# Attention block on one core: x kept in a ring of six buffers, gamma and beta rows broadcast by TensorE, the maxima pass one slot later over 65 rows, stacks without zero rows

## The reference

```python
def _sln(h, w, ln_g, ln_b, Wg, bg, Wb, bb):
    mu = jnp.mean(h, axis=-1, keepdims=True)
    var = jnp.mean((h - mu) ** 2, axis=-1, keepdims=True)
    ln = (h - mu) / jnp.sqrt(var + EPS) * ln_g + ln_b
    return (w @ Wg.T + bg)[:, None, :] * ln + (w @ Wb.T + bb)[:, None, :]
h = _sln(hidden, w, ...)                       # hidden: (16, 256, 256)
qkv = (h @ Wqkv.T + bqkv)                      # q, k, v: 16 heads x 16 features
energy = jnp.einsum('bhqd,bhkd->bhqk', q, k)
att = jax.nn.softmax(energy, axis=-1) / D ** 0.5
out = jnp.einsum('bhqk,bhkd->bhqd', att, v) ... @ Wp.T + bp
h1 = out + hidden
return _sln(h1, w, ...) + h1
```

## Time and profile before

| | |
|---|---|
| median of 3 runs | 408.3 us (407.98 to 411.03) |
| profiled execution | 412.25 us, its span 410.4 us |
| mean granted clock of TensorE | 0.967 |
| busy in the span | PE 88%, DVE 73%, ACT 57%, POOL 30% |
| DMA queue of SP | 53.11 MB, 78.7% of 16 engines |

### The profile page before, as it was taken

How to read it: one execution, slowest core, us unless ns; L and a number is a source line. 1 busy time by engine, 2 the same in 40 slices (tenths; PEclk the granted TensorE clock), 3 DMA queues, 4 the chain that set the end, 5 groups by cost and what they waited for, 6 DMA issues and landing times.

```text
span 410.4 us, 8984 instructions
## 1 busy us (share of the span) xinstructions
PE 359.5 (88%) x3208; PEld 300.6 (73%) x3209; DVE 298.1 (73%) x730; ACT 235.5 (57%) x437; POOL 121.6 (30%) x108
## 2 busy tenths in 40 slices
PE   3856579798989999998999899999899999988972
PEld 3636478687878788887878687878787888857652
DVE  7714738476878788786878787887787886977454
ACT  8320227466666767575657566665667575755750
POOL 5310403142415142332424242424142323030332
PEclk9986969899999999999999999999999999999996
DMA  6179895969598799969897969899979989590221
GB/s 206 37 96 127 116 106 103 162 100 161 115 174 114 157 158 128 186 108 181 119 192 109 180 112 180 126 175 121 174 123 124 168 108 181 101 184 10 81 78 51
DMA packets 50334, 53.68 MB, mean 131 GB/s; under 512 B 6610, under 2 KB 41825, under 8 KB 50290
## 3 DMA queue, kind: packets, MB, share of 16 engines
q1 hardware_dynamic: 50290, 53.11, 78.7%
HBM read 14.18 MB, written 4.23 MB: 45 GB/s over the span
## 4 chain that ended last, share of the span: by engine, by line
PE 49%; DMA 22%; SPq 18%; DVE 5%; issue 4%; ACT 1%; POOL 1%; POOLq 0%; DVEq 0%
DMA kst<-qk_l 19%; PE m L689 16%; SPq L288 15%; PE st L689 11%; PE sa L689 9%; PE pv L689 9%; DMA qst<-m_l 2%; SPq L291 2%; PE pv L784 2%; DVE mx L489 1%; DVE qst L640 1%; PE pv L837 1%; PE pv L798 1%; SPq L301 1%; DVE y L600 0%
## 5 line engine op out<-in xcount | busy, mean ns | idle before, releaser
L489 DVE TENSOR_REDUCE mx<-sa 128x2 f32<-128x512 f32 x256 | 174.3, 683 | 90.6 <-PE sa L689 86.3
L467 ACT ACTIVATE p<-st 128x512 f32<-128x512 f32 x256 | 150.5, 597 | 101.8 <-PE st L689 99.6
L689 PE MATMUL sa<-kst,qst 128*128 128x256 f32 x512 | 107.8, 294 | 31.9 <-DMA kst<-qk_l 31.1
L689 PE MATMUL st<-qst,kst 128*128 128x256 f32 x512 | 112.8, 303 | 1.4 <-ACT p L467 0.7
L689 PEld LDWEIGHTS sa<-kst,qst 128*128 128x128 f32 x512 | 80.5, 194 | 37.8 <-DMA kst<-qk_l 28.0
L689 PEld LDWEIGHTS st<-qst,kst 128*128 128x128 f32 x512 | 79.6, 193 | 23.2 <-ACT p L467 15.2
L689 PE MATMUL pv<-p,v_st 128*32 128x256 f32 x1024 | 68.5, 385 | 0.3 <-ACT p L467 0.3
L357 POOL TENSOR_TENSOR hT_l<-hT,hT_h 128x512 fp32r<-128x512 f32 x16 | 20.6, 1285 | 100.3 <-ACT hT_h L400 100.3
L371 POOL TENSOR_TENSOR rstd<-vare,minus_half 128x4 f32<-128x4 f32 (+1 forms) x21 | 18.8, 893 | 95.5 <-DVE vare L544 92.0
L376 POOL TENSOR_TENSOR h1b<-h,gb 128x512 f32<-128x512 f32 x16 | 20.6, 1285 | 87.2 <-DVE h L573 87.2
L689 PEld LDWEIGHTS pv<-p,v_st 128*32 128x32 f32 x1024 | 26.7, 109 | 20.2 <-ACT p L467 0.5
(11 more groups left out here) (95 smaller groups left out, 537.2 us busy)
## 6 DMA issues: line engine op xcount, KB each, us to landing
qst<-qk_h SPq DMA_DIRECT2D x64, 128.0 KB
qst<-qk_l SPq DMA_DIRECT2D x64, 128.0 KB
kst<-qk_h SPq DMA_DIRECT2D x64, 128.0 KB
kst<-qk_l SPq DMA_DIRECT2D x64, 128.0 KB
xa<-x_dram SPq DMA_DIRECT2D x16, 256.0 KB, 4.0
xd<-x_dram SPq DMA_DIRECT2D x16, 256.0 KB, 3.4
gb<-gb_rows SPq DMA_DIRECT2D x16, 256.0 KB, 3.7
out_dram<-y SPq DMA_DIRECT2D x16, 256.0 KB, 4.0
```

Of the source, the lines that this page charges most:

```text
L467: nc.scalar.activation(p32[:, h % PR, :], st_ps[h % 2][:], ACT.Exp).then_inc(exp_done, 1)
L489: dve.tensor_reduce(mx[:, par(a), h // HH, (h % HH) * TT:(h % HH + 1) * TT], sa_ps[h % 2][:].rearrange("p (t n) -> p t n", t=TT), AX.X, AL ...
L689: return nc.tensor.matmul(o, l, r, start=start, stop=stop)
```

## The change

- `xa` becomes a ring of six images (`NX = 6`, `xbuf(a)`). POOL adds the bias in it, DVE's L573 reads it, and the second load of x (`xd`) goes.
- The rows of gamma and beta stay on chip. They are split into a high and a low part in `gb_hl` (16 rows each). In slot 3 of a step (`S_GB`) PE multiplies them with `pick_b`, a 0/1 matrix that POOL makes for each image in its slot 2, into `pv_ps[0]`: the row, broadcast to 128 partitions. ACT copies it to `gb` in slot 4. POOL's `h1b` goes from slot 1 to slot 6, `xn` from slot 5 to 7. The DRAM round trip and the `gb` DMAs go.
- `LEAD` goes: slot h holds `scores_max(b+1, h)`.
- Row 64 of `qst` is zero for good and rows 65 and 66 hold the maxima. The maxima pass contracts over 65 rows, the scores pass over 67. So the clearing DMA goes (`NSTK = 8`), as do the clearings of 128-row stacks at the start; four DMAs at the start write the fixed rows.

```diff
-ROWS = 4 * HD + 2
+ZERO_ROW = 4 * HD
+ROWS = ZERO_ROW + 3
-NSTK = 9
+NSTK = 8
+NX = 6
@@ sync
-            sp.dma_start(raw(kst[4 * HD:ROWS]).rearrange("r p h n -> r (p h n)"), ones[:]).then_inc(ones_in, 16)
-            sp.wait_ge(gbrow_ready, 1)
-            sp.dma_start(gb_dram, gbrow[:]).then_inc(gb_out, 16)
-            sp.wait_ge(gb_out, 16)
+            for r in range(ZERO_ROW, ROWS):
+                sp.dma_start(raw(kst[r:r + 1]).rearrange("a p h n -> a (p h) n"),
+                             ones[0:2 * H, :]).then_inc(fixed_rows_in, 16)
+            sp.dma_start(raw(qst[ZERO_ROW:ZERO_ROW + 1]).rearrange("a p h n -> a (p h) n"),
+                         zrows[:]).then_inc(fixed_rows_in, 16)
+            sp.wait_ge(gbl_ready, 1)
+            sp.dma_start(raw(gb_hl[B:2 * B, :]), raw(gb_l[:])).then_inc(gbl_in, 16)
...
-                if t == 0:
-                    sp.dma_start(raw(qst[4 * HD:ROWS, p, g * HH:(g + 1) * HH, :]), zrows[:]).then_inc(s, 16)
...
                 if has(b + 4):
                     wait(sp, xn_ready, 1 * (b + 2) + 1)
-                    sp.dma_start(xa[:, par(b + 4)], x_t[b + 4]).then_inc(x_in[par(b + 4)], 16)
+                    wait(sp, h1_ready, 1 * (b - 2) + 1)
+                    sp.dma_start(xbuf(b + 4), x_t[b + 4]).then_inc(x_in[par(b + 4)], 16)
...
-                if has(b):
-                    wait(sp, y_ready, 1 * (b - 2) + 1)
-                    sp.dma_start(xd[:, par(b)], x_t[b]).then_inc(xd_in[par(b)], 16)
-                    sp.dma_start(gb[:, par(b)], gb_dram[b]...broadcast_to([P, 2 * D])).then_inc(xd_in[par(b)], 16)
@@ gpsimd
-                    if h == 1 and has(b - 2):
+                    if h == 2 and has(b - 2):
+                        wait(pool, gb_done, 1 * (b - 3) + 1)
+                        pool.tensor_copy(pick_b[:], pick[:, b - 2:b - 1].broadcast_to([P, P])).then_inc(pick_b_ready, 1)
+                    if h == 6 and has(b - 2):
+                        wait(pool, gb_ready, 1 * (b - 2) + 1)
                         wait(pool, h1_ready, 1 * (b - 2) + 1)
...
-                    if h == 5 and has(b + 3) and not first(b + 3):
+                    if h == 7 and has(b + 3) and not first(b + 3):
                         norm_x(b + 3)
...
-            pool.memset(raw(kst[:, 0]), 0.0).then_inc(pad_k_zero, 1)
@@ scalar
+                    if h == S_GB + 1 and has(b - 2):
+                        wait(act, gb_done, 1 * (b - 2) + 1)
+                        wait(act, y_ready, 1 * (b - 3) + 1)
+                        nc.scalar.activation(gb[:], pv_ps[0][:], ACT.Copy).then_inc(gb_ready, 1)
...
-            for pad in (kst, qst):
-                nc.scalar.activation(pad[:, 1]..., ones[:, 0:1]..., ACT.Copy, scale=0.0).then_inc(pad_1_zero, 1)
@@ vector
-                    i = h + LEAD
-                    maximum(b + 1 + i // H, i % H)
+                    maximum(b + 1, h)
...
-            dve.memset(raw(qst[:, 0]), 0.0).then_inc(pad_v_zero, 1)
@@ tensor
-                    o = mm(sa_ps[h % 2][:, t * N:(t + 1) * N], qst[:, p, h, t * P:(t + 1) * P],
-                           kst[:, p, h, :], True, True)
+                    o = mm(sa_ps[h % 2][:, t * N:(t + 1) * N], qst[0:ZERO_ROW + 1, p, h, t * P:(t + 1) * P],
+                           kst[0:ZERO_ROW + 1, p, h, :], True, True)
...
-                    i = h + LEAD
-                    scores_max(b + 1 + i // H, i % H)
+                    scores_max(b + 1, h)
...
+                    if h == S_GB and has(b - 2):
+                        ...
+                        wait(pe, pick_b_ready, 1 * (b - 2) + 1)
+                        wait(pe, ml_ready, 2 * min(b, B - 1) + 2)
+                        wait(pe, att_ready, 2 * min(b - 1, B - 1) + 1)
+                        mm(pv_ps[0][:], pick_b[:], gb_hl[:], True, True).then_inc(gb_done, 1)
```

More of the change, by code:

```diff
@@ L477, in _ @@
             nc.scalar.activation(wp_h[:], wp[:], ACT.Copy).then_inc(wph_ready, 1)
-            steps(step)
+            steps(step, last=B + 2)
         @block.vector
```

96 lines of the change are left out of this document (50 added, 46 removed).

## The result

The changed kernel takes **417.62 us** (median of 4 runs, 417.31 to 421.39) where the kernel before took 409.24 in runs beside it (407.98 to 411.03): 1.0233 times as long, 95% interval 1.0193 to 1.0274. The forecast of 398.3 has the wrong sign, and its range, to 405.5, does not hold the result. The profiled execution took 417.91 us with a span of 416.1, against 412.25 and 410.4.

A forecast was written before the change was run, and what follows sets the result against it. Taken as bound: each step's chain through the stack DMAs and PE, with PE stalled about 1 us. 2.5 + 7.15 (13 x 0.55) + 0.8 + 1.6 - 0.5 - 1.15 - 0.4 = 10.0: 408.3 to 398.3 us, range 391.5 to 405.5.

The forecast's parts named there:

- Fewer rows: PE's products over fewer rows: rows don't shorten a product and no reason to take longer; bounds 0 and 0.
- (b): Steady step: the removed clearing DMA had made a few engines lag; 0.55 us a step gained, bounds 0.2 and 1.0.
- only an even share: Rival: engines shared the clearing evenly, so 0.2 instead of 0.55 a step; 403.3 us, chance 0.18.
- (a): Steady step, T to m_l: m_l lands 0.35 behind the stacks' 11.15; the new order gains 0.70 and loses this.
- (c): Steady step, first st to next T: 10.72 becomes 10.36, with 0.24 for the new product and 0.10 for slower start.
- Edits at nothing: Steady step: x and gb loads, ACT's copy, the new product's DVE wait, pick_b, later xn and fewer rows cost nothing.
- The ends: Lead-in and exit outside the steady steps: gains of 2.5, 0.8 and 1.6, losses of 0.5, 1.15 and 0.4.
- Lead-in: Before the steady steps: clearings go, gT and wqkv_l start earlier, one sa pair fewer ahead of the projections; 2.5 gained.
- Exit: Step 14: its st starts at T + 10.95 instead of T + 11.76 (0.8); head 8's sa wait of 1.61 goes (1.6).
- The last `y` behind `h1b`: At the end: rstd runs ahead of h1b, the last y needs both and starts 1.15 us later.
- Maxima in place of stacks: Rival: m_l, bound by its queue place, still lands at T + 11.5; step 21.86, time near 405.5; chance 0.12.
- The rivals: PE alone 393.7 (0.2), even share 403.3 (0.18), maxima near 405.5 (0.12), late gb 402.2 (within forecast's 0.5).

The follow-up runs named there:

- rows66: Kernel before with both the maxima and the score products contracted over 66 rows instead of 128, nothing else changed; 418.39 us, 1.0196.
- filled_66: lead_off_filled with both the maxima and the score products over 66 rows instead of 128; 403.42 us, 0.9867.
- fill14: Changed kernel with seven products of zeros ahead of the first score product of step 14, where PE paused for m_l; 416.1 us, 1.0109.
- filled: bias_wait with products of zeros in PE's pauses: before the first maxima product, in steps 0 and 1, in slots 0 and 8 of step 14; 408.06 us, 0.9946.
- filled_late: filled, with SP also waiting for both weight transfers before it issues the four fixed-row DMAs; 404.36 us, 0.9864.
- stacks_only: Kernel before with only the new stacks: eight DMAs, 65 and 67 rows, no clearings, fixed rows written after the weights, maxima slot as before; 412.73 us, 1.0063.
- no_clear: lead_off_filled without the DMA that clears the maxima rows, exponent of 0 times the scores, for times only; 404.27 us, 0.9878.
- lead_back: Changed kernel with the maxima of a head a slot earlier again (LEAD = 1 on PE and DVE); 418.53 us, 1.017.
- lead_off_filled: lead_off with the same products of zeros in PE's pauses as filled; 128 rows and nine DMAs a stack stay; 402.18 us, 0.9824.
- bias_wait: Changed kernel with POOL's bias add held until DVE's first y product of slot 8 is done; 411.68 us, 1.0046.
- gb_ahead: Changed kernel with gamma and beta made one image earlier into two buffers, POOL's h1b in slot 1 and xn in slot 5 again; 418.66 us, too scattered for a ratio.
- ring_only: Kernel before with only the ring of six for x in place of the second load; 411.9 us, 1.0024.
- lead_off: Kernel before with only the slot move of the maxima (LEAD gone on PE and DVE); 408.61 us, 0.9947.
- rows_only: Kernel before with the maxima products contracted over 64 rows and the score products over 66 instead of 128; 506.37 us, 1.2187.
- st128: Changed kernel with fixed-row DMAs after the weights and score products over 128 rows again, ACT and POOL clearing the added rows in the lead-in; 418.82 us, 1.0233.

## Why the prediction was wrong

**Fewer rows, "bounds 0 and 0": this step failed, and by the stretches of the profiled spans it is the larger part of what makes the kernel slower.** I read from the earlier trace rows that rows don't shorten a product, and the result agrees: the products stayed as long. But the row cannot show what the rows do to the clock. rows66, with no other edit, is 8 us slower and has 23.9 us at half clock where the kernel before has 3.4. The prediction named the clock only in its last sentence, as a thing that would make it wrong, with no price, and took 1.00 in the earlier trace rows as a state and not as something that the work upholds. In the changed kernel the clock's share is the +1.44 of step 0 and most of the +3.05 of step 14. Shown: the rows matter where pauses stand (rows66 against filled_66), and with filled pauses the clock stays up (fill14 in part, filled, filled_late). Not settled: how the chip weighs rows and pauses.

**(b) The clearing DMA, 0.55 a step: failed, with 7.15 us the largest term of the sum.** stacks_only finds 0.07 us between T and `sa`, no_clear no gain at all. I built the lag from two completions 0.75 apart and 19 late packets; the lag may be there, but it is not the clearing's. The chain stood on the transfer, and there the even share of 0.13 was the better reading. This was the rival "only an even share" or less. What makes a few engines late is still open.

And yet the last stack does land earlier in the changed kernel. lead_back, which waits for it at `sa` as the kernel before does, starts that `sa` at T + 10.69 on average (10.48 to 10.97) where the kernel before needs 11.11; the forecast was 10.60. Neither the clearing (11.04) nor the second load of x (11.09) does that alone. Whether it is the `gb` DMA or all three together, no run shows. In the changed kernel itself the last stack lands at T + 10.68, but `m_l` 0.68 behind it, not 0.35: 0.35 to 0.8 in ten steps and 1.3 to 1.5 in the other three. That is what the steady step lacks, 21.75 instead of 21.31, and why those three fall out is open too.

By the rule of the Trainium skill, "DMA: Bandwidth & Descriptors", section "Why a DMA increments its semaphore by 16 and not by 1", on how many engines carry a DMA, I had put up to 1.0 us on this term. No run here shows such a gain when the DMA of two partitions is gone.

**(a) The joint, 0.35: right.** In lead_off_filled, which has this and no other part of the change, the step is 21.51 against 21.87, 0.36 less. **(c) 10.36: right**, 10.37 measured. It holds a cost of 0.24, the product that makes `gb`, and this takes back what the earlier landing gives: in filled_late `m_l` lands at T + 11.16, in lead_off_filled at T + 11.34, and their steps are 21.58 and 21.51.

**"Edits at nothing": failed at POOL.** I followed `xn`, 1.26 later behind `h1b`, to its reader on PE and stopped, and did not ask what stands behind `xn` on POOL itself. The bias add does, and it came to lie on DVE's `y`, with `aT_l` and the issue of `m_l` behind that. In the steady step this costs nothing that the runs can tell; at the end it costs 2.4 us. bias_wait, which keeps them apart, is 6 us faster than the changed kernel; that is between rounds, 1.0046 against 1.0233 of the same kernel before, and 4.4 in the profiled spans (416.1 and 411.7). Of this only the 2.4 are traced to the overlap, and gb_ahead, which parts them too, is no faster than the changed kernel in three of its four executions. The second load of x was rightly costed at nothing (ring_only), but the 1.5 us earlier start of the other stacks that I drew from them hardly shows: the wait of slot 8 in step 14 is 1.41 in ring_only against 1.61.

**The ends.** Lead-in: `gT` did move, to 9.85, but I had costed none of the four new DMAs that stand ahead of the stacks, and they hold the second weight back: `wp` takes 10.3 us to land instead of 6.4. With them out of the way T of step 0 is 3.0 us earlier than before (62.15 against 65.19), so the 2.5 was a fair size. Exit, 0.8 and 1.6: the first fails with `m_l`, as in the steady step; the second was wrong in kind, since the wait of slot 8 does not go but passes to `m_l`, 1.76 us in fill14, where the clock lets it be seen. The last `y` behind `h1b`, 1.15: 1.20 measured. Step 15 ahead of it took 1.14 more where the sum had 0.65; there `y` is beside POOL again, beside `h1b` and the bias add, 2.27 for a pair in DVE's timeline where the kernel before has 1.36 beside the bias add alone:

```profile
402.19 2.27 DVE L601 SCALAR_TENSOR_TENSOR y<-h,mv,gb 128x256 f32<-128x256 f32 x2
```

**The rivals.** None of the four was the cause of the loss. "Maxima in place of stacks" describes the steady step well: it had `m_l` at T + 11.5 and a step of 21.86, and 11.36 and 21.75 were measured. It left a gain at the ends, though, 405.5 in all, and the loss of 5.7 us lies there and in step 0: in the clock, in the weights and in POOL's order. No rival spoke of any of these.

## What to carry to other kernels

When a change moves one instruction on an engine, follow the whole list behind it on that engine, and ask of each what it will now overlap; a POOL instruction and a two-input DVE one are a pair to keep apart where DVE ends last (1.44 us against 0.87 here). Then ask whether the thing made late is awaited: `m_l` was issued 0.57 later and landed no later, behind a full queue. Read such times over all steps, not in one. Price the clock like an instruction: where PE pauses, note what the change does to the pause and to the rows of the products around it, and try a few idle products in the pause, which took the ratio from 0.9947 (lead_off) to 0.9824 (lead_off_filled) here. Before a DMA is called late because of its neighbour, take the neighbour out in one run.

## What was not expected of the hardware

**Rows and the clock.** The same order of work with 66 rows instead of 128 had 23.9 us at half clock between 60 and 390 us (6.8 + 3.4 + 13.7) where the kernel before had 3.4. In rows_only PE was busy without a gap and the clock stayed low, in the windows:

```profile
40.00:150.00 110.00, 109.52 (x454) 80.15 (x458) 44.76 (x100) 33.86 (x63) 15.75 (x14) 0.50 0.52 76
```

The Trainium skill, "TensorE: Matmul & The Clock Gate", section "What's actually happening", says that the ratio of the gate is set by how busy PE has been. This row disagrees, or busy there means more than issued products: 109.52 us of 110 were busy, at 0.50.

**64 rows are another form.** The same three rows of PE's timeline, with the maxima products at 66 rows (rows66) and at 64 (rows_only):

```profile
304.90 0.50 PE L689 MATMUL st<-qst,kst 66*128 66x256 f32 x2
305.24 0.40 PE L689 MATMUL sa<-kst,qst 66*128 66x256 f32 x2
305.48 0.28 PE L689 MATMUL m<-ones_r,rows 128*128 128x256 f32 x1
```

```profile
305.22 0.50 PE L689 MATMUL st<-qst,kst 66*128 66x256 f32 x2
305.65 0.50 PE L689 MATMUL sa<-kst,qst 64*128 64x256 f32 x2
306.08 0.39 PE L689 MATMUL m<-ones_r,rows 128*128 128x256 f32 x1
```

From `st` to the projection it is 0.58 with 66 rows and 0.86 with 64, 0.28 more in this slot, and the step at full clock went to 25.75 (299.58 - 196.57 over four). The Trainium skill, "TensorEngine Tiling (Array Packing)", section "Tiling Modes", puts 64 rows in another mode of the array and says that a switch of mode drains it; the trace agrees. The changed kernel's 65th row of zeros, which looks like waste, keeps it out of this: its `sa` pairs over 65 rows take 0.40.

**DVE behind POOL.** Not only two-input instructions stand behind POOL: the copy of a single row in st128 took 6.54 us beside two memsets. The trace does not show whether the same lock is the reason.
